# A modulated attention and FFN layer in one kernel: a rewritten opening, and the residual of all eight token tiles on VectorE

## The reference, cut to what matters

```python
mod = (silu(c) @ wmod).reshape(4, 6, 1, 512)
sa, ca, ga, sb, cb, gb = (mod[:, i] for i in range(6))
ga = (2 * (ga >= 0) - 1) * maximum(abs(ga), 0.25)      # gb likewise
h = layernorm(x) * (1 + ca) + sa                       # x: (4 batches, 256 tokens, 512)
x = x + ga * attention(h)                              # the first residual
h = layernorm(x) * (1 + cb) + sb
x = x + gb * ffn(h)                                    # 512 -> 1376 -> 512, silu gate
```

## Time and profile before

| | us |
|---|---|
| median of 3 executions | 1086.44 (1085.96 to 1086.52) |
| the profiled execution's own time | 1084.36 |
| its span, first to last instruction | 1082.4 |
| PE busy | 1029.5 (95%) |
| DVE busy | 796.9 (74%) |
| ACT busy | 707.8 (65%) |
| POOL busy | 228.7 (21%) |
| mean granted TensorE clock | 0.991 |

### The profile page before, as it was taken

How to read it: one execution, slowest core, us unless ns; L and a number is a source line. 1 busy time by engine, 2 the same in 40 slices (tenths; PEclk the granted TensorE clock), 3 DMA queues, 4 the chain that set the end, 5 groups by cost and what they waited for, 6 DMA issues and landing times.

```text
span 1082.4 us, 14473 instructions
## 1 busy us (share of the span) xinstructions
PE 1029.5 (95%) x4668; PEld 805.0 (74%) x4668; DVE 796.9 (74%) x1560; ACT 707.8 (65%) x1381; POOL 228.7 (21%) x141
## 2 busy tenths in 40 slices
PE   4989899999999999999999999999999699999898
PEld 2767577777777877777777777777777367888686
DVE  5785788888788878888887888788887896334322
ACT  3445787888788778878887887788777565233300
POOL 2321122211231122222111221121232640000000
PEclk9899899999999999999999999999999999999999
DMA  8407310131122013101311230122031303111011
GB/s 307 137 25 79 117 39 21 39 117 45 33 83 90 19 39 113 42 19 39 116 39 27 89 97 19 39 94 61 19 98 59 97 20 127 59 39 59 20 39 39
DMA packets 41724, 72.00 MB, mean 67 GB/s; under 512 B 7328, under 2 KB 23968, under 8 KB 39648
## 3 DMA queue, kind: packets, MB, share of 16 engines
q1 hardware_dynamic: 40832, 71.21, 21.7%
q10 hardware_dynamic: 864, 0.43, 0.1%
HBM read 69.38 MB, written 2.24 MB: 66 GB/s over the span
## 4 chain that ended last, share of the span: by engine, by line
PE 86%; DVE 7%; DMA 3%; ACT 2%; issue 1%; SPq 1%; POOL 0%; DVEq 0%; ACTq 0%
PE ps_q_gt L68 14%; PE ps_q_gt L70 14%; PE ps_q_gt L69 14%; PE ps_o L68 5%; PE ps_o L70 5%; PE ps_o L69 5%; PE ps_s L789 5%; PE ps_kv_x L70 3%; PE ps_kv_x L69 3%; PE ps_kv_x L68 3%; PE ps_kv_x L812 2%; PE ps_y L798 2%; DMA dec<-gT_dram 2%; PE ps_ss L820 1%; PE ps_y L806 1%
## 5 line engine op out<-in xcount | busy, mean ns | idle before, releaser
L1818 POOL TENSOR_TENSOR q_sin<-q_sin,cst 128x512 f32<-128x512 f32 x64 | 88.4, 1381 | 315.5 <-ACT q_sin L964 315.5
L1533 DVE SCALAR_TENSOR_TENSOR prob<-ps_s,scal,dec 128x128 f32<-128x128 f32 x256 | 71.9, 343 | 79.3 <-PE ps_s L789 79.3
L1806 POOL TENSOR_TENSOR dec<-dec,future 128x1024 f32<-128x1024 f32 x31 | 74.5, 2404 | 255.3 <-ACT expg L983 255.3
L68 PE MATMUL ps_q_gt<-hT_hi,wq_hi 128*128 128x512 f32 x256 | 125.6, 491 | 0.0
L68 PE MATMUL ps_o<-wo_hi,z_hi 128*128 128x512 f32 x260 | 103.4, 398 | 1.0 <-DVE z_lo L63 0.9
L68 PE MATMUL ps_q_gt<-hT_hi,wg_hi 128*128 128x512 f32 x256 | 103.3, 403 | 0.0
L70 PE MATMUL ps_o<-wo_hi,z_lo 128*128 128x512 f32 x260 | 102.5, 394 | 0.0
L69 PE MATMUL ps_o<-wo_lo,z_hi 128*128 128x512 f32 x260 | 102.4, 394 | 0.0
L69 PE MATMUL ps_q_gt<-hT_lo,wg_hi 128*128 128x512 f32 x256 | 100.6, 393 | 0.0
L70 PE MATMUL ps_q_gt<-hT_hi,wq_lo 128*128 128x512 f32 x256 | 100.6, 393 | 0.0
L70 PE MATMUL ps_q_gt<-hT_hi,wg_lo 128*128 128x512 f32 x256 | 100.1, 391 | 0.0
(11 more groups left out here) (286 smaller groups left out, 2643.3 us busy)
## 6 DMA issues: line engine op xcount, KB each, us to landing
dec<-gT_dram SPq DMA_DIRECT2D x32, 512.0 KB, 5.5
raw_q<-wq_in SPq DMA_DIRECT2D x32, 256.0 KB, 2.7
raw_g<-wg_in SPq DMA_DIRECT2D x32, 256.0 KB, 2.9
raw_o<-wo_in SPq DMA_DIRECT2D x8, 1024.0 KB, 6.1
raw_pair<-wkv_in SPq DMA_DIRECT2D x8, 512.0 KB, 4.6
raw_pair<-wgu_in SPq DMA_DIRECT2D x7, 512.0 KB, 3.2
raw_gu<-wgu_in SPq DMA_DIRECT2D x6, 512.0 KB, 3.3
qT<-wmod_in SPq DMA_DIRECT2D x2, 1024.0 KB, 6.1
```

The costliest lines, as they stand in the source:

```text
L68: pe.matmul(out, w_hi, x_hi, start=first, stop=False)
L1533: last = nc.vector.scalar_tensor_tensor(prob[:, h], ps_s[:, h * P:(h + 1) * P], scal[:, tile, 1, h:h + 1], dec[:, tile // 2 % 2, h, tile % ...
L1806: nc.gpsimd.tensor_tensor(cells, cells, future[:].unsqueeze(1).broadcast_to([P, GRP * CPB, CHUNK]), ALU.add).then_inc(mask_done, 1)
L1818: nc.gpsimd.tensor_tensor(q2, q2, sinT, ALU.mult).then_inc(qsin_done, 1)
```

## The change: what it does

**SP.** x's first half is loaded ahead of SA and CA, and the second half behind them. GA is issued once SA's rows are there and ahead of the rotary tables, GB after head 1; SB, head 2, CB and head 3 follow, each behind its own wait. Zeros come to `x1` by two DMAs of 1 MB from `wo_hi` (which POOL has set to zero), where POOL's memset is gone. The gate values are stored as 16 rows of 128 values, from `gate_rows`, and SP waits for that store to land before it goes into the loop.

```diff
+            sp.wait_ge(rows_ready, KT * len(MODS))
+            for half in range(2):
+                a = half * NT // 2
+                sp.dma_start(x1[:, a:a + NT // 2], wo_hi[:].bitcast(F32)).then_inc(zeros_done, 16)
             for i in range(2):
                 sp.wait_ge(gT_copied, i + 1)
                 sp.dma_start(gT_dram[:, i * HALF:(i + 1) * HALF], gT[i]).then_inc(gT_stored, 16)
...
-            sp.wait_ge(guard, GUARD_END)
+            sp.wait_ge(gate_copied, 1)
             for i in range(2):
-                sp.dma_start(modrow[i].rearrange("(m p) -> p m", p=P),
-                             gate_T[:, i].rearrange("p b k -> p (b k)"),
-                             allow_slow_non_contiguous=True).then_inc(rows_stored, 16)
+                sp.dma_start(modrow[i].rearrange("(m p) -> m p", p=P),
+                             gate_rows[:, i * P:(i + 1) * P]).then_inc(rows_stored, 16)
+            sp.wait_ge(rows_stored, 32)
```

```diff
+    def scalar_modulate(self, act, b):
+        act.wait_ge(self.turned, b + 1)
+        if b >= 2:
+            act.wait_ge(self.lo_done, b - 1)
         for k in range(KT):
+            last = self.nc.scalar.activation(
+                self.hf[:, b % 2, k].rearrange("p (c i) -> p c i", c=CPB),
+                self.ps[b][:, :, k * P:(k + 1) * P], ACT.Identity,
+                bias=self.shift[:, k, b:b + 1], scale=self.scale[:, k, b:b + 1])
...
+    def vector_split_hi(self, dve, b):
+        dve.wait_ge(self.hf_done, b + 1)
+        split_hi(self.nc.vector, self.hT_hi[:, :, b * L:(b + 1) * L], self.hf[:, b % 2]).then_inc(self.hi_done, 1)
```

**PE** has a new order in the opening, and two new transposes, `gate_turn`:

```diff
             mod_rows(SA)
+            mod_turn(0)
             mod_rows(CA)
-            mod_turn(0)
+            pe.wait_ge(cst_loaded, 16)
+            norm.tensor_turn(pe, 0)
             mod_turn(1)
-            pe.wait_ge(cst_loaded, 16)
+            norm.tensor_turn(pe, 1)
+            pe.wait_ge(norm.lo_done, 1)
+            kv_batch(0, -1)
             pe.wait_ge(modT_done, 2)
-            for t in range(6):
-                norm.tensor_turn(pe, t)
-            pe.wait_ge(norm.lo_done, CPB)
-            kv_batch(0, -1)
-            norm.tensor_turn(pe, 6)
-            norm.tensor_turn(pe, 7)
-            pe.wait_ge(norm.lo_done, NT // 2)
+            norm.tensor_turn(pe, 2)
+            pe.wait_ge(win_split, 2)
+            pe.wait_ge(norm.lo_done, 2)
+            softplus_argument(0)
+            pe.wait_ge(norm.hf_done, 2)
+            norm.tensor_turn(pe, 3)
             q_block(0, -4, True)
             g_block(0, -4, 0, KT, True)
             k_turn(0, -1)
...
             q_block(0, -1)
-            mod_turn(5)
+            gate_turn()
             g_block(0, -1, 0, KT)
+            pe.wait_ge(gate_copied, 1)
             pe.wait_ge(late_modT_done, 2)
```

**The residual** of tiles 0 to 4 moves from POOL to DVE:

```diff
             def dve_residual(t):
-                n = t - POOL_TILES
+                dve.wait_ge(ga_loaded, 16)
                 dve.wait_ge(sums_done, KVH * NT - (NT - 1) + t + 1)
-                scale_sum(nc.vector, 1, t)
-                add_x(nc.vector, dve, 1, t, n)
+                nc.vector.tensor_tensor(x1[:, t], x1[:, t], grow[:, t // CPB], ALU.mult).then_inc(scaled, 1)
...
+                nc.vector.tensor_tensor(x1[:, t], x1[:, t], x_again[t], ALU.add).then_inc(residual, 1)
...
-            groups(dve, step, lambda t: None)
+            def between(t):
+                if t in (2, 3):
+                    dve_residual(t - 2)
+
+            groups(dve, step, between)
             ln_stats(0)
...
             rotate_k(g, 2, 4)
+            dve_residual(2)
             ln_stats(2)
             normed_z(g, 4)
             copy_scalars(g, 2)
+            dve_residual(3)
             ln_stats(3)
...
             split_z_lo(g, 5)
+            dve_residual(4)
             dve.wait_ge(plo_done, g * 8 + 7)
             probabilities(g, 7)
...
-            groups(pool, step, between)
-            residual_tile(2)
+            groups(pool, step, lambda t: None)
             split_w_lo(0)
-            residual_tile(3)
             mask(KVH - 1, 2)
             split_w_lo(1)
             ln_lo(0)
-            residual_tile(4)
             ln_lo(1)
             split_w_lo(2)
```

More of the change, by code:

```diff
@@ L104, with __init__ @@
 class Norm:
[L109 to L112, removed]
+    def __init__(self, ctx, nc, rows, x1, hT_hi, hT_lo, shift, scale, ident, banks, hf):
         def sem(name):
-            return ctx.enter_context(nc.semaphore(name + tag))
+            return ctx.enter_context(nc.semaphore(name))
         self.nc, self.x1, self.hT_hi, self.hT_lo = nc, x1, hT_hi, hT_lo
@@ L119, in __init__ @@
         self.stats, self.mv, self.var, self.rstd = rows
[L120 to L126, removed]
+        self.hf, self.ps = hf, banks
         self.stats_done = sem("stats_done")
@@ L173, in bank @@
[L173 to L179, removed]
-        for k in range(KT):
[L181 to L189, removed]
-        for k in range(KT):
-            last = self.nc.scalar.activation(self.hf[:, t % self.hf_slots, k], self.bank(t)[:, k], ACT.Identity,
-                                             bias=self.shift[:, k, b:b + 1],
-                                             scale=self.scale[:, k, b:b + 1])
-        last.then_inc(self.hf_done, 1)
@@ new lines, in _ @@
+            norm.scalar_modulate(act, 0)
+            split_kv_hi(0)
+            split_head_hi(0, 0)
+            norm.scalar_modulate(act, 1)
+            norm.scalar_rstd(act, 1)
+            split_head_hi(0, 1)
+            copy_v(0, -1)
+            norm.scalar_modulate(act, 2)
+            copy_zT(0)
+            norm.scalar_modulate(act, 3)
+            swap(0, -4, True)
+            split_head_hi(0, 2)
+            exp_gate(0, -4)
+            copy_kT(0, -1)
+            sigmoid(0, -4)
@@ new lines, in _ @@
+            copy_zT(1)
+            copy_rows(2)
+            act.wait_ge(chain, CHAIN_ABS)
+            nc.scalar.activation(za, za, ACT.Exp, scale=-1.0).then_inc(exp_done, 1)
+            exp_gate(0, -3)
+            copy_rows(3)
+            split_head_hi(0, 3)
+            swap(0, -3)
+            sigmoid(0, -3)
+            copy_rows(4)
+            copy_rows(5)
+            swap(0, -2)
+            exp_gate(0, -2)
+            sigmoid(0, -2)
+            copy_gT(0)
+            act.wait_ge(cum_ready, 1)
@@ new lines, in _ @@
+            nc.scalar.activation(tok[:, :, 0], ps_z, ACT.Copy, scale=-1.0).then_inc(exp_done, 1)
+            copy_gT(1)
+            act.wait_ge(chain, CHAIN_DIFF)
+            nc.scalar.activation(zs, zs, ACT.Exp).then_inc(exp_done, 1)
+            swap(0, -1)
+            act.wait_ge(gate_turned, 1)
+            nc.scalar.activation(gate_rows, ps_y[0:B * KT, 0:2 * P], ACT.Copy).then_inc(gate_copied, 1)
+            act.wait_ge(mod_turned, len(MODS))
+            exp_g(0, -1)
+            exp_gate(0, -1)
@@ new lines, in _ @@
+            norm.vector_split_hi(dve, 2)
+            norm.vector_split_hi(dve, 3)
+            rotate_q_cos(0, -4)
+            split_head_lo(0, 2)
+            cap(0, -4)
+            rotate_q_add(0, -4)
+            gate(0, -4)
+            softplus_before_exp()
+            softplus_argument_of_series()
+            cap(0, -3)
+            softplus_series(0)
+            rotate_q_cos(0, -3)
+            gate(0, -3)
+            softplus_series(1)
+            rotate_q_add(0, -3)
+            decay_rates()
@@ L1833, in _ @@
                 .then_inc(future_done, 1)
-            for t in range(NT):
-                norm.pool_split_lo(pool, t)
+            for b in range(B):
+                norm.pool_split_lo(pool, b)
             pool.wait_ge(tables_loaded, 16)
```

336 lines of the change are left out of this document (130 added, 206 removed).

## The result

The changed kernel takes 1073.30 us (median of 4 runs, 1071.97 to 1075.40), the one before 1086.48 us (4 runs): a ratio of 0.988, 95% interval 0.986 to 0.990. The forecast was 1070.7, in a range of 1065.5 to 1076.5. The profiled execution took 1072.09 us with a span of 1070.0, against 1084.36 and 1082.4: 12.4 us less, where the working had 15.7.

The account below looks back on a forecast made before the run. PE bounds the kernel (busy 1029.5 of 1082.4 us), so only its idle, half-clocked or delayed stretches can give; DVE bounds late in the last group. -9.2 - 7.0 + 0 + 0.5 = -15.7, from 1086.44 to 1070.7 us, range 1065.5 to 1076.5.

Parts of the forecast that it names:

- Part 1, the gate store: First steps of group 0: storing gates by rows removes the wait for `dec` and the half clock behind it, -9.2 us.
- Part 2, the opening: Before the loop: kv_batch starts at 26.05 instead of 28.85, scores at 75.1 instead of 82.05, -7.0 us.
- rival 1: The opening gives only its earlier start, -2.8 instead of -7.0 us, total 1075; chance 0.14.
- Part 3, zeros: Zeros by two SBUF-to-SBUF DMAs late in the opening, landed at 66, needed at 75: cost nothing.
- Part 4, the residual: Last group: residual of five tiles moved from POOL to DVE, +0.5 us in sum at 879.68.
- Step 3: Last group's loop step 3: with tile 0's residual on DVE, squares come at 842.9 against 843.50, -0.6 us.
- The tail: 844 to 880 us, DVE the bound: four more residual tiles add 5.2, relief from POOL's blocking offsets part, +1.1 us.
- the normalisation: Tail, DVE at 856.80: two normalisations take about 1.0 instead of 3.99 with POOL quiet, up to 3.0 us saved.
- the smaller blocks: Tail, DVE before 880: half a dozen smaller blocks by POOL's residuals go, worth some 2 us.
- one of the signs: From the loop's entry to PE's last wait in the tail it should take 788.9 +- 2 us.
- The base: The earlier runs' median, 1086.44, lies 2.1 us above their profiled execution; that gap was carried over whole.

Follow-up runs that it names:

- the other order: Changed kernel with VectorE's gated output of loop step 4 and its low part ahead of the residuals of tiles 2 and 3; tail 39.52 us, 1.16 longer.
- before + new store: The kernel before with only the gates' row store new (two transposes, ScalarE's copy, store by rows); 1079.25 us, 8.2 under the kernel before in the same round.

## Why the prediction was right, and by how much not

**Part 1, the gate store: mechanism right, -9.2 measured as -7.4.** From the scores of step 0 to the y product of step 2 it is 106.31 - 75.09 = 31.22, not 29.51. The store's stall and the half clock behind it went entirely; what was missed is a new half clock right behind the entry, from 2.41 us of idling. Where PE was kept busy there, the same measure is 29.56 and entry to step 3 is 9.0 under the kernel before (737.98 against 747.02). I had seen that PE idles at the entry (2.00) and that half clock follows an idle stretch (114 to 116), and didn't ask what the first would do to the second. That is +1.7 in the profiled execution, and 0 or +1.7 from run to run. It is not all the change's doing: the kernel before idles there as well, and its profiled execution had drawn full clock.

**Part 2, the opening: -7.0, and -6.96 measured.** kv_batch at 25.50 (26.05 forecast), 47.18 us of PE's work (47.15), the entry at 75.09. No rival 1. The mechanism is as forecast; that the two agree to 0.04 us is luck, since the same opening enters the loop at 74.65 to 75.64 in other executions, and kv_batch starts at 25.3 to 26.8 in them.

**Part 3, zeros: cost 0, as measured.** They land at about 63 (66 forecast). What the step didn't see is that the memset, left in the new order, would have cost 3.5 to 4.

**Part 4, the residual: +0.5 forecast, +2.0 measured.** Two sizes were off. Step 3 gave -0.2 instead of -0.6: PE's wait of 3.36 became two, 1.31 for the gate and 1.49 for the squares, and the residual of tile 0 held VectorE for 4.6 us (818.78 to 823.37) where 4.3 had been reckoned; where the rest of the difference lies I don't know. The tail gave +2.15 instead of +1.1. DVE's busy time from the probabilities of step 4 to the last low part went from 33.28 in 34.80 us to 35.98 in 36.90, so +2.7 less 0.6 of idling. Of the +2.7, 5.2 is the four tiles, -3.0 the normalisation (1.00 instead of 3.99), both as forecast; about -1.7 the smaller blocks (2 forecast), and +2.15 the residual of tile 2 under GpSimd's mask and split, for which I had 1.0. (The 0.65 between a tile's two starts was misread: they are 0.71 apart, and the next instruction comes 0.61 later, so a tile is 1.3 all the same.) Timelines of DVE and of POOL there:

```profile
836.45 0.68 DVE L1609 BATCH_NORM_STATS2 stats<-x 128x6 f32<-128x512 f32 x1
...
841.76 1.00 DVE L1636 TENSOR_SCALAR xn<-x,mv,rstd 128x512 f32<-128x512 f32 x2
...
845.52 2.83 DVE L1617 TENSOR_TENSOR x<-x,raw_o 128x512 f32<-128x512 f32 x1
...
854.12 3.06 DVE L1636 TENSOR_SCALAR xn<-x,mv,rstd 128x512 f32<-128x512 f32 x2
```

```profile
835.24 2.41 POOL L62 TENSOR_TENSOR wgu_lo<-raw_pair,wgu_hi 128x1024 fp32r<-128x1024 f32 x1 [12.41 <-ACT wgu_hi L1157]
842.95 2.36 POOL L1795 TENSOR_TENSOR dec<-dec,future 128x1024 f32<-128x1024 f32 x1 [5.31 <-ACT expg L969]
845.26 2.54 POOL L62 TENSOR_TENSOR wgu_lo<-raw_gu,wgu_hi 128x1024 fp32r<-128x1024 f32 x1
853.62 2.82 POOL L62 TENSOR_TENSOR hT_lo<-hf,hT_hi 128x1024 fp32r<-128x1024 f32 x1 [5.82 <-DVE hT_hi L57]
```

The block of 3.06 at 854.12 stands in all versions but that of the other order (3.09 in the kernel before, 2.58 there), so the change gained nothing by it. The rule of the Trainium skill that I had weighed ("SBUF — State Buffer", "Who interferes with whom") held in its second half too, where a run shows it: the statistics of 836.45, which started under GpSimd's split of 835.24, took 0.68 us, as when it is quiet.

**The sum.** -6.96 - 7.42 - 0.18 + 2.15 + 0.01 = -12.40. The 3.3 us less than forecast are the half clock (1.7) and the residual (1.5). So one of the signs failed: from the entry to the last wait of PE in the tail it took 792.3 us, where 788.9 +- 2 had been named. The base was carried over 2.1 above the profiled execution; the changed kernel's median is 1.2 above its own, which brought 0.9 back. That is luck: by how much a median lies above its profiled execution is set by which idle stretches drew half clock.

## What to carry to other kernels

Cut every execution at the same points of the program before reading totals: here the stages behind the entry repeat to 0.3 us, draws of the clock apart, while medians hide an effect of 1.7 us behind draws of 1.6. Where TensorE idles some 2 us at a known place, fill it with products that nobody reads, or take away the wait. And cost work that moves between VectorE and GpSimd by which engine is the bound at that place, tile by tile: the same edit gained at most 0.5 us in one step and lost 2.0 to 2.3 in the next.

## What was not expected of the hardware

- 2.00 us of idling were enough for a fall to half clock (at 84.40 in "before + new store"), and 2.56, in the kernel before even 3.06 and 3.36, passed without one. Nothing in the program tells the two apart; here 28 of 46 stretches of 2.0 to 2.6 us were followed by it.
- A memset on GpSimd, which reads nothing, blocked a 128x32 VectorE operation with its one input in SBUF for its whole length: 4.30 us. The two of the same width just ahead, which read `ps_s_y`, ran through in 0.18 under GpSimd's q_sin. Nor is every operation with one input in SBUF held up: the statistics of 836.45 in the changed kernel were not.
- Two stores of 8 KB in single values slowed a load of 512 KB in another engine's queue from 5.6 to 14.7 us, and one of 1 MB from 4.8 to 17.7.
